# Two-layer graph attention kernel: two of each chunk's eight moves go from ScalarE's queue to GpSimd's, and the loads of adj the other way

## The reference

```
for l in range(2):
    proj = x @ W[l]; Wh, Ws = split(proj, 2, axis=-1)
    scores = Wh @ Ws.T
    a = softmax(scores, axis=-1) * adj
    x = leaky_relu(a @ Wh + x, 0.01)
out = layernorm(x0 + x)        # x0: the input
```

## Time and profile before

| | |
|---|---|
| median of 3 runs | 1690.79 us (1690.45 to 1693.78) |
| profiled execution, its own time | 1689.17 us |
| its span | 1687.3 us |
| TensorE clock granted, mean | 0.989 |
| PE busy | 1594.6 us (95%) |
| DVE busy | 1231.2 us (73%) |
| POOL busy | 916.3 us (54%) |
| ACT busy | 676.5 us (40%) |
| DMA, 16 engines | 179 GB/s mean |

### The profile page before, as it was taken

One profiled execution on the slowest core, in us unless ns is written; L12 is line 12 of the kernel. 1 busy time (PEld: TensorE's weight loads), 2 busy tenths in 40 slices (PEclk: granted clock), 3 DMA queues, 4 the chain that ended last, 5 costly groups with the idle time before them and its releaser, 6 DMA issues.

```text
span 1687.3 us, 23469 instructions
## 1 busy us (share of the span) xinstructions
PE 1594.6 (95%) x8104; PEld 1324.0 (78%) x8104; DVE 1231.2 (73%) x1558; ACT 676.5 (40%) x1175; POOL 916.3 (54%) x935
## 2 busy tenths in 40 slices
PE   7889999999999999999688999999999999999996
PEld 6778888888788888888577888888888888878785
DVE  4667777767777777777535788778878887788785
ACT  4244444444444444444323443444343444443442
POOL 2355555555555555555353555555555655555565
PEclk9999999999999999999889999999999999999999
DMA  5357767787678777777713677777777777767774
GB/s 181 85 144 184 196 184 183 184 206 184 183 181 198 184 184 186 190 190 208 215 55 91 175 186 191 197 187 190 189 196 202 188 193 196 191 180 187 194 204 130
DMA packets 167750, 302.59 MB, mean 179 GB/s; under 512 B 39760, under 2 KB 68432, under 8 KB 167504
## 3 DMA queue, kind: packets, MB, share of 16 engines
q1 hardware_dynamic: 106192, 133.28, 32.4%
q0 software_dynamic: 36864, 134.23, 27.9%
q10 hardware_dynamic: 24576, 33.59, 8.3%
HBM read 157.29 MB, written 9.44 MB: 99 GB/s over the span
## 4 chain that ended last, share of the span: by engine, by line
PE 58%; DVE 20%; POOL 7%; ACTq 6%; ACT 5%; issue 3%; DMA 1%; SPq 0%; POOLq 0%
PE banks L410 19%; PE banks L309 10%; PE banks L311 9%; PE banks L310 9%; PE banks L412 9%; DVE neg_max L601 7%; DVE ring L629 6%; POOL a_lo L727 6%; ACTq L215 6%; DVE ring L634 4%; ACT a_hi L522 3%; ACT ring L503 1%; DVE weight L620 1%; DVE wh L565 1%; DVE x_t L565 1%
## 5 line engine op out<-in xcount | busy, mean ns | idle before, releaser
L727 POOL TENSOR_TENSOR a_lo<-turned,a_hi 128x512 fp32r<-128x512 f32 x512 | 716.9, 1416 | 687.4 <-ACT a_hi L522 687.1
L410 PE MATMUL banks<-wh,a_hi 128*128 128x512 f32 x2048 | 754.8, 407 | 56.0 <-POOL a_lo L727 49.4
L503 ACT ACTIVATE ring<-banks,neg_max 128x1024 f32<-128x1024 f32 x256 | 286.0, 1117 | 798.4 <-DVE neg_max L601 798.4
L412 PE MATMUL banks<-wh,a_lo 128*128 128x256 f32 x2048 | 578.4, 282 | 0.0
L410 PEld LDWEIGHTS banks<-wh,a_hi 128*128 128x128 f32 x2048 | 388.7, 190 | 189.8 <-POOL a_lo L727 85.8
L601 DVE TENSOR_REDUCE neg_max<-banks 128x1 f32<-128x1024 f32 x256 | 311.0, 1215 | 270.0 <-PE banks L311 270.0
L309 PE MATMUL banks<-x_t,q_t 128*128 128x512 f32 x1024 | 406.1, 397 | 5.6 <-DVE x_t L565 4.0
L311 PE MATMUL banks<-x_t,q_t 128*128 128x512 f32 x1024 | 402.5, 393 | 0.0
L310 PE MATMUL banks<-x_t,q_t 128*128 128x512 f32 x1024 | 401.4, 392 | 0.0
L412 PEld LDWEIGHTS banks<-wh,a_lo 128*128 128x128 f32 x2048 | 390.9, 191 | 6.1
L629 DVE SCALAR_TENSOR_TENSOR ring<-ring,weight,load 128x1024 f32<-128x1024 f32 x256 | 372.3, 1454 | 4.9 <-DMA load<-adj 2.4
(11 more groups left out here) (66 smaller groups left out, 743.1 us busy)
## 6 DMA issues: line engine op xcount, KB each, us to landing
load<-adj POOLq DMA_DIRECT2D x256, 512.0 KB, 5.0
turned<-ring SPq DMA_DIRECT2D x1536, 64.0 KB, 4.0
turned<-ring ACTq DMA_DIRECT2D x512, 64.0 KB, 4.1
ring<-x SPq DMA_DIRECT2D x8, 512.0 KB, 4.9
rows<-x SPq DMA_DIRECT2D x32, 128.0 KB, 4.1
x_scratch<-rows SPq DMA_DIRECT2D x32, 128.0 KB, 4.0
ring<-x_scratch SPq DMA_DIRECT2D x8, 512.0 KB, 4.9
rows<-x_scratch SPq DMA_DIRECT2D x32, 128.0 KB, 4.3
```

What stands on the lines that cost most here:

```text
L410: nc.tensor.matmul(psum[:, bank, :], a_hi[:, s, b], wh[:, k].rearrange("p a d -> p (a d)"), start=start, stop=stop, skip_group_check=True)
L412: last = nc.tensor.matmul(psum[:, bank, 0:D], a_lo[:, s, b], wh[:, k, 0], start=False, stop=stop, skip_group_check=True)
L503: nc.scalar.activation(ring[:, i % RING, :].rearrange("p (b e) -> p b e", b=2), psum[:, 2 * (i % 2):2 * (i % 2) + 2, :], ACT.Exp, bias=neg ...
L727: nc.gpsimd.tensor_tensor(a_lo[:, j % 2].rearrange("p b (r j) -> p b r j", r=QUADS), as_f32(turned[:, unit % 2, :, b:b + SUB, :]).rearrang ...
```

## The change

The two moves that ACT issued for each chunk, those of rows group r = 2 and r = 3 of the second half q = 1, are issued by POOL, behind its two subtractions of the step. They wait for `blocks_turned` where POOL waited for `a_done`. ACT issues the load of `adj` in their place, behind its exponentials, with the wait for `a_done`. POOL's moves count on semaphores of their own, so that each wait for a chunk's moves takes three semaphores where it took two: ahead of the exponentials 3 for 2, ahead of a pair of chunks' first `a_hi` 6 for 4. The first two loads of `adj` are issued by ACT too.

```diff
+        pool_moved = [[sem(f"pool_moved{u}_{q}") for q in range(QUADS)] for u in range(2)]
...
+        def wait_moved(engine, i):
+            u, c, of = i // 2 % 2, i % 2, i // 4 + 1
+            engine.wait_ge(moved[u][2 * c], 64 * of)
+            engine.wait_ge(moved[u][2 * c + 1], 32 * of)
+            engine.wait_ge(pool_moved[u][2 * c + 1], 32 * of)
...
-        SP_MOVES, ACT_MOVES = chunk_moves[:6], chunk_moves[6:]
-
-        def move(queue, i, moves):
+        SP_MOVES, POOL_MOVES = chunk_moves[:6], chunk_moves[6:]
+
+        def move(queue, i, moves, signals):
...
-                                ).then_inc(moved[u][to], 16)
+                                ).then_inc(signals[u][to], 16)
...
@@ ScalarE
-            def move_blocks(i):
-                act.wait_ge(blocks_turned, i + 1)
-                if i >= 4:
-                    act.wait_ge(lo_done, SUB * (i // 2 - 1))
-                move(nc.scalar, i, ACT_MOVES)
...
+            act.wait_ge(w_next_stored, 32)
+            for i in range(2):
+                load_adj(nc.scalar, i)
...
                 m = chunk_at(step - LAG_WEIGH)
-                if m is not None:
-                    move_blocks(m)
+                if m is not None and m + 2 < LAYERS * CHUNKS:
+                    act.wait_ge(a_done, m + 1)
+                    load_adj(nc.scalar, m + 2)
...
@@ GpSimd
-            pool.wait_ge(w_next_stored, 32)
-            for i in range(2):
-                load_adj(nc.gpsimd, i)
...
                 m = chunk_at(step - LAG_WEIGH)
-                if m is not None and m + 2 < LAYERS * CHUNKS:
-                    pool.wait_ge(a_done, m + 1)
-                    load_adj(nc.gpsimd, m + 2)
+                if m is not None:
+                    pool.wait_ge(blocks_turned, m + 1)
+                    if m >= 4:
+                        pool.wait_ge(lo_done, SUB * (m // 2 - 1))
+                    move(nc.gpsimd, m, POOL_MOVES, pool_moved)
```

More of the change, by code:

```diff
@@ L251, in move_blocks @@
                     sp.wait_ge(lo_done, SUB * (i // 2 - 1))
-                move(sp, i, SP_MOVES)
+                move(sp, i, SP_MOVES, moved)
             load_w(0)
@@ L286, in _ @@
                         i = CHUNKS - RING + (x_slot(g) - CHUNKS) % RING
-                        for q in range(2 * (i % 2), 2 * (i % 2) + 2):
-                            sp.wait_ge(moved[i // 2 % 2][q], 64 * (i // 4 + 1))
+                        wait_moved(sp, i)
                         for p in range(2):
@@ L496, in exponentials @@
                 if i >= RING:
-                    m = i - RING
-                    for q in range(2 * (m % 2), 2 * (m % 2) + 2):
-                        act.wait_ge(moved[m // 2 % 2][q], 64 * (m // 4 + 1))
+                    wait_moved(act, i - RING)
                 elif i % RING >= W_SLOT:
@@ L514, in split_a @@
                 if b == 0:
-                    for q in range(QUADS):
-                        act.wait_ge(moved[unit % 2][q], 64 * (unit // 2 + 1))
+                    for i in (2 * unit, 2 * unit + 1):
+                        wait_moved(act, i)
                 if j % SUBS < 2:
```

## The result

The changed kernel takes 1730.62 us (median of 4 runs, 1725.21 to 1732.14), against 1692.28 us (1690.45 to 1696.09) for the kernel before, run beside it: a ratio of 1.0218, 95% interval 1.0188 to 1.0247. It is 38 us slower; forecast were 41. The profiled execution has a span of 1728.6 us, 41.3 more than before, at a granted clock of 0.985 against 0.989.

The account below looks back on a forecast made before the run. PE, busy 95%, was bound by its 49.4 us wait for POOL's low parts at tile boundaries. 61 x 0.71 = 43 us less some 2 gave +41: 1689.17 to 1730 profiled, 1732 as median; range 1676 to 1744.

Parts of the forecast that it names:

- The sum: Whole kernel: 61 x 0.71 = 43 us, less some 2 us for ACT's long issues, gives +41 us.
- The bound and the chain: Tile boundary: PE's 49.4 us wait for `a_lo`, behind factors, row weights, weighing, next maximum, exponentials and `a_hi`.
- ACT's part: ACT behind the exponentials: `a_hi` starts 0.17 and 0.33 us earlier; 0.45 us a tile taken, 27 us over 61 tiles.
- The tie: Tile boundary: POOL's first piece and DVE's L620 both start at 2.02; POOL goes first, chance 0.50, 1732 us.
- The rival of a tie that goes to DVE: Tile boundary: DVE goes first, only 15 tiles with late `inv_std` are blocked; 1681 us, chance 0.15.
- The price of a blocked L620: Tile boundary: L620 waiting for POOL's first piece, and the weighing for both, costs 1.21 us a tile.
- The net 0.71: Each blocked tile: 1.21 us lost less 0.17 and 0.33 us from the earlier starts of `a_hi`.
- No block at all: Tile boundary: L620 unhindered by start order, or L670 ahead without delay; 27 us faster, 1664 us, chance 0.13.
- POOL's moves: POOL's queue, each step: two moves at 0.58 us for one issue add 0.58 us, covered by slack; cost nothing.
- `inv_std`: 15 layer-2 tiles with a query piece: `inv_std` 0.58 us later, L620 at about 2.4 or 2.5, blocked whatever a tie does.
- A late `adj`: Load of `adj` in blocked tiles: some land a few tenths late; nothing taken, upper bound 30 us.
- The 2 us for ACT's long issues: ACT's queue: a guessed gain of some 2 us from removing its moves' rare long issues, up to 2.46 us.

Follow-up runs that it names:

- the form that isn't blocked: Changed kernel with the weight operation L620 written to also sum its output into a spare column, against the kernel before: 1654.87 us, ratio 0.9775.

## Why the prediction was right, step by step

The mechanism and its place were as forecast, and the time nearly so: 1732 predicted, 1730.62 measured. That the two agree to 1.4 us is partly luck, since errors of several us in the terms cancel (see "The sum").

**The bound and the chain: right.** The added time is in PE's wait for `a_lo`, 98.1 us instead of 49.4, and it arises at the tile boundary alone.

**ACT's part: right in effect, its term too large.** The load's issue takes 0.33 us in the median (0.6 was taken, bounds 0.37 to 0.62), but either ends under the exponentials, so `a_hi` comes at 1.29 and 1.10, as forecast from the earlier trace rows. By itself it was put at 27 us. With the form that isn't blocked it measured 37: that tile takes 24.06 us instead of 24.63, a gain of 0.57 where 0.45 was taken. The full sum of the two earlier starts, 0.50, was nearer, and POOL's start came 0.03 us earlier still.

**The tie: right, and less of a tie than forecast.** POOL starts 0.70 and not 0.73 behind `a_hi`, and so 0.01 ahead of the weight operation. The bounds of L629, borrowed for L620 (POOL wins 0.04 us late, loses 0.08 late), hold: blocked at gaps of 0.02 to 0.05 and free at 0.07 in kernels that differ by the length of one row sum, with POOL idle until its subtraction. The rival of a tie that goes to DVE was to decide from a start of `a_hi` at 1.35 on; it did at 1.39, and gave 1658, not 1681, as the layer-2 tiles had been freed as well.

**The price of a blocked L620: right.** 1.21 us from one row; the next exponentials came 1.06 us later, and tiles are 1.26 us longer than with the form that isn't blocked (25.32 against 24.06). The net 0.71 measured 0.69 and 0.72: price and gain were each some 0.05 us too low. The Trainium skill (SBUF — State Buffer, "Who interferes with whom") lets whoever issues first hold the port pair, and the trace agrees at gaps from 0.07 us on where POOL was idle before its subtraction; below, by the recorded starts, the order is not kept. It also exempts the VectorE form that writes out an accumulator: the run of that form agrees, with 0.22 us beside a running subtraction.

**No block at all: refuted** for this form of instruction, by 59 of 61 boundaries.

**POOL's moves: hidden at most places, and not free.** A move takes 0.50 us in the median (0.58 was taken), and the usual tile shows nothing of it. What "cost nothing" missed stands under "The sum". All instructions of the line in the changed kernel, with those of ACT's loads:

```profile
L224 POOL DMA_DIRECT2D turned<-ring x512: 496/498/667, 55.9 to 1709.0; - x171
...
L213 ACTq DMA_DIRECT2D load<-adj x256: 333/334/445, 26.4 to 1696.3; - x128
```

**`inv_std`: right in direction, wrong in size, and with an effect that was not seen.** Timelines of POOL and DVE at the end of a tile with a query piece in layer 2, to set beside the earlier trace rows:

```profile
1193.41 0.57 POOL L758 TENSOR_TENSOR inv_std<-var_eps,minus_half 128x1 f32<-128x1 f32 x1
1194.70 2.55 POOL L733 TENSOR_TENSOR a_lo<-turned,a_hi 128x512 fp32r<-128x512 f32 x2 [0.73 <-ACT a_hi L528]
```

```profile
1192.71 0.16 DVE L612 TENSOR_REDUCE row_neg_max<-neg_max 128x1 f32<-128x4 f32 x1
1194.01 0.41 DVE L676 TENSOR_SCALAR rows<-rows,moments,inv_std 128x256 f32<-128x256 f32 x1 [1.14 <-POOL inv_std L758]
1194.92 1.10 DVE L626 TENSOR_SCALAR weight<-factor,row_inv 128x4 f32<-128x4 f32 x1
```

`inv_std` ends at 1.27 (1.42 forecast) and L626 starts at 2.21 (2.4 to 2.5 forecast), 0.22 us behind POOL: blocked whatever happens in a tie, as said. That is so at 14 boundaries (15 were forecast). At two more, which end tiles without a query piece, POOL's moves and `inv_std` behind them came later still, and L676 itself ran into POOL's pair. One of them:

```profile
1317.21 2.59 POOL L733 TENSOR_TENSOR a_lo<-turned,a_hi 128x512 fp32r<-128x512 f32 x2
...
1317.27 1.38 DVE L676 TENSOR_SCALAR rows<-rows,moments,inv_std 128x256 f32<-128x256 f32 x1 [2.02 <-POOL inv_std L758]
1318.57 1.24 DVE L619 TENSOR_TENSOR scaled_sum<-factor,chunk_sum 128x4 f32<-128x4 f32 x1
```

There the first row operation waits for POOL's second piece; at the other boundary L676 waits for both (2.62 us). L626 is free but starts at 5.14 and 6.05, and the tiles that follow take 26.40 and 27.39 us. They are the two of the 61 where L626 wasn't blocked.

**A late `adj`: refuted.** The loads land in 4.4 us (5.0 before) and DVE waited 4.3 us for them in the whole execution.

**The sum.** 43 us for the tiles stands against 41.3 of span, but other terms cancel in it. Three tiles of the changed kernel are 7.4 us longer together than their like: 28.15 us (exponentials at 456.67), 26.40 and 27.39 (the two above). In the first and the last POOL's moves start late although nothing in the profile holds them:

```profile
466.83 1.01 POOL L224 DMA_DIRECT2D turned<-ring  x2 [5.62 <-issue]
...
1662.16 1.01 POOL L224 DMA_DIRECT2D turned<-ring  x2 [2.12 <-issue]
```

The same chunks (the 65th, 126th, 187th and 248th) have moves that start 1.6 to 3.5 us late in every profile here with the moves on POOL and the load on ACT. So it comes with the change, and the forecast had it at nothing; its cause is open. Against it, 4.5 us were won ahead of the first blocked boundary and between the layers. The 2 us for ACT's long issues was a guess, and no run isolates it.

## What to carry to other kernels

When an instruction is made to start earlier, ask what it will now meet, and compare the two start times on the shared resource to a hundredth: here 0.17 us won on one engine put a 0.23 us operation behind a 1.3 us one, and a gain of 37 us turned into a loss of 38. A tiny operation at the head of a chain is worth as much care as a large one: take it off the path, give it a form that isn't blocked, or make sure of a gap. And a gain that fails can be one instruction away: undo or alter the suspected instruction alone before the whole change is given up.

## What the runs showed that was not expected

- By the records, a tensor_scalar of 128x4 that starts up to 0.05 us ahead of GpSimd's subtraction still waits for it, at all boundaries of two kernels; from 0.07 us on it did so at one boundary in each alone, where GpSimd was still issuing its moves when it started. In the kernel before with the later weights it was blocked at gaps up to 0.054 and free at 0.055. That the records begin before the port is claimed would explain it; this was not tested.
- Of two operations in line behind POOL's first piece, the one already waiting goes first. If DVE's weighing waits there it passes ahead of POOL's second piece (the summing form, POOL's pair 3.52 us); if the tiny weight operation waits there, POOL's second piece comes ahead of the weighing (2.54 us). So a blocked tiny operation costs its engine the wait for two pieces, not for one.
- A blocked boundary can cost twice its own 1.2 us: in the kernel before with the later weights PE's wait was followed at 19 of 48 blocked tiles by 3.4 us at half of the granted clock, and such tiles were 2.71 us longer than before instead of 1.22.
- A DVE tensor_tensor of 128x4 with two inputs in SBUF was blocked too (1.24 us where it takes 0.16), while the row sums were not (0.16 us beside the subtractions, at 14 boundaries of the run with the moves alone). The same section of the Trainium skill says both: two inputs in SBUF contend with a GpSimd instruction that reads SBUF, and tensor_reduce never does.
